# Gated-attention loop on one core: residual adds on GpSimd, half of every second turned copy on ScalarE, moments one step later

## The chip, the cores and the metric

One Trainium2 chip, of which one core is used. A core has TensorE (PE: matmuls, its weight loads are listed as PEld), VectorE (DVE), ScalarE (ACT), GpSimd (POOL) and SyncE (SP, which issues the DMAs here); they run their own instruction streams, in order, and meet at semaphores. The metric is the device time of one execution of the whole kernel in microseconds (us), as a median of runs. Durations come from one profiled execution, whose trace lists every instruction by engine and by line of the kernel.

## What is computed

Four blocks in a row, each with a residual and a layer norm: a linear attention, a gated attention with one shared key and value head per token, a decay attention and a grouped attention with a routed mixture of experts. The change lies in the second:

```python
gating = softmax(x @ W_gate.T); idx = argmax(gating)          # 16 heads
k_shared, v_shared = key head idx, value head idx * max(gating)
att = einsum('bhqd,bkd->bhqk', q, k_shared) / sqrt(hd)         # hd = 16
att = softmax(where(causal, att, -inf))
y = einsum('bhqk,bkd->bhqd', att, v_shared)
x = layernorm(x + y)
```

There are 4 batches of 256 tokens and 256 features, so 1024 tokens in 8 tiles of 128.

## The kernel before

`layer0_gated_attention` first makes the gates, picks keys and values (token tiles `kv_tok`), and spreads and turns the keys. Its main part is a loop over 32 steps of two heads each (8 steps per batch) and two loops of overhang; each engine has its own copy of the loop, written out by hand, and the order in an engine's copy is the order of its queue. For step `n`:

- PE writes a causal mask (`masks`, L942) and scores (`scores`, L956 and L958) of both heads into two PSUM banks, 0 and 1 or 2 and 3 in turn.
- DVE takes the negated maxima of the rows (`maxima`, L785 and L786).
- ACT takes four exponentials into `probs` (`exps`, L868).
- PE turns the probabilities with six transposes (`turn`, L949) into banks 4 and 5, one bank per head, two loops later: loop `n` turns step `n - 2`.
- DVE copies both banks to `probsT` (`copy_turned`, L791), also two loops later. There are 4 buffers of `probsT`, but only one pair of banks, so the next turn waits for the copy.
- In every even loop PE multiplies two steps' turned probabilities with the values (`values`, L968 and L970); a column of ones in the values gives the sum of the probabilities.

Every fourth loop ACT copies a half batch of results out (`copy_out`, L874), and at the loops `out_at(b, t)`, which are 12, 14, 20, 22, 29 and 30 for the first three batches, PE turns a token tile of results (`turn_outputs`, L978) and DVE runs `outputs`: a reciprocal (L797), the product with it (L799) and the sum with the residual `x` into `y` (L801). Right behind each, DVE takes the moments of that tile for the next norm (L547). The norm of the first four tiles runs inside the loop as well: variance in loop 22 (L553, L561), its power on POOL (L615), factors and products in loop 24, and transposes, high and low parts in loops 25 to 28.

POOL makes paddings and prepares weights of the next layer (`following.prepare`), then only the power. Behind the loop ACT loads the Silu table (L892), evaluates queries of the next layer (L1140, L1142) and copies the last results out, for whose transposes PE waits. The last two tiles have their `outputs` there. A barrier ends the block; the next layer starts behind it.

Of the kernel before, what the change touches and what calls it, by code (L numbers as in the profile page):

```python
# [23 lines left out]
ALU = mybir.AluOpType  # L24
ACT = mybir.ActivationFunctionType
# [5 lines left out]
BATCH, SEQ, D = 4, 256, 256  # L31
# [3 lines left out]
TPB = SEQ // P  # L35
CAUSAL = 384

H0, HD0 = 16, 16
# [63 lines left out]
def need(eng, sem, value):  # L102
    if value > 0:
        eng.wait_ge(sem, value)
# [556 lines left out]
def layer0_gated_attention(c, norm, following, next_norm, later_norm):  # L661

    nc, ps = c.nc, c.ps
# [4 lines left out]
    STEPS = BATCH * PER  # L668
# [3 lines left out]
    with ExitStack() as ctx:  # L672
        def sb(name, shape, dt=F32):
# [20 lines left out]
            ctx, "g", "z_ps lg_ps kv_ps q_ps kT_ps s_ps t_ps pv_ps o_turned")  # L694
        z_ready, picked_ps, kv_ready, nm_ready, pT_ready, rs_ready, o_scaled, chain = c.sems(
            ctx, "g", "z_ready picked_ps kv_ready nm_ready pT_ready rs_ready o_scaled chain")
        z_copied, e_ready, q_ready, k_ready, kT_ready, p_ready, o_ready = c.sems(
            ctx, "g", "z_copied e_ready q_ready k_ready kT_ready p_ready o_ready")
        c.finished += pe_sems
        block = ctx.enter_context(nc.Block())  # L700

# [2 lines left out]
        def out_at(b, t):  # L704
            return PER * b + (13 + t if b == 2 else 12 + 2 * t)
# [22 lines left out]
        @block.gpsimd  # L728
        def _(pool):
            norm.split(pool, 1)  # L730
            pool.memset(kv_tok[:], 0.0).then_inc(padded, 1)
            pool.memset(k_pad[:], 0.0).then_inc(padded, 1)
            pool.wait_ge(padded, 1)
            pool.memset(kv_tok[:, :, 1, HD0:HD0 + 1], 1.0).then_inc(padded, 1)
            following.prepare(pool)
            next_norm.power(pool)

        @block.vector
        def _(dve):
            norm.moments(dve, range(6, NT))  # L740
            norm.variance(dve, 1)
            norm.factors(dve, 1)
            norm.apply(dve, 1)
            norm.low(dve, 1)
            link = Chain(dve, chain)

            z, e, cand, one_hot, top_hot, eq = (gate[:, n] for n in range(6))
            nmax, esum, emax, erec, top, first = (gstat[:, n] for n in range(6))

            def wide(a):  # L750
                return a.unsqueeze(2).broadcast_to((P, NT, H0))

            dve.wait_ge(lg_ps, 1)
            logits = ps[:, 0, 0:NT * H0].rearrange("p (t h) -> p t h", t=NT)
            link(dve.tensor_reduce(nmax, logits, X, ALU.max, negate=True))
            dve.tensor_tensor(z, logits, wide(nmax), ALU.add).then_inc(z_ready, 1)
            dve.wait_ge(e_ready, 1)
            dve.tensor_reduce(esum, e, X, ALU.add)
            link(dve.tensor_reduce(emax, e, X, ALU.max))
            link(dve.reciprocal(erec, esum))  # L760
            dve.tensor_tensor(top, emax, erec, ALU.mult)

            link(dve.tensor_tensor(eq, e, wide(emax), ALU.is_equal))
            link(dve.scalar_tensor_tensor(cand, eq, -16.0, c.iota.unsqueeze(1).broadcast_to((P, NT, H0)), ALU.mult, ALU.add))
            link(dve.tensor_reduce(first, cand, X, ALU.min))
            link(dve.tensor_tensor(one_hot, cand, wide(first), ALU.is_equal))
            link(dve.tensor_tensor(top_hot, one_hot, wide(top), ALU.mult))
            dve.wait_ge(padded, 3)

            def pick(t):  # L770
                dve.wait_ge(kv_ps, t + 1)
                kv = kv_bank(t).rearrange("p (a h d) -> p a h d", a=2, h=H0)
                for a, hot in enumerate((one_hot, top_hot)):
                    mul = dve.tensor_tensor(picked[:, t % 2, a], kv[:, a], hot[:, t, :].unsqueeze(2).broadcast_to((P, H0, HD0)), ALU.mult)
                mul.then_inc(picked_ps, 1)

            def gather(t):
                dve.wait_ge(picked_ps, t + 1)
                dve.tensor_reduce(kv_tok[:, t, :, 0:HD0], picked[:, t % 2].rearrange("p a h d -> p a d h"), X, ALU.add).then_inc(kv_ready, 1)

            def maxima(n):
                dve.wait_ge(s_ps, n + 1)
                need(dve, p_ready, n - 3)
                pair = ps[:, banks(n):banks(n) + 2, :]
                dve.tensor_reduce(neg_max[:, n % 4, 0], pair[:, :, 0:P], X, ALU.max, negate=True)  # L785
                dve.tensor_reduce(neg_max[:, n % 4, 1], pair[:, :, P:CAUSAL], X, ALU.max, negate=True).then_inc(nm_ready, 1)  # L786

            def copy_turned(n):
                dve.wait_ge(t_ps, n + 1)
                need(dve, pv_ps, (n - KEPT_T) // 2 + 1)  # L790
                dve.tensor_copy(probsT[:, n % KEPT_T], ps[:, 4:6, 0:CAUSAL]).then_inc(pT_ready, 1)  # L791

            def outputs(b, t):
                seq = TPB * b + t
                turned = out_bank(b, t).rearrange("p (h r) -> p h r", h=H0)
                dve.wait_ge(o_turned, seq + 1)
                dve.reciprocal(rsum[:, t, :], turned[:, :, HD0]).then_inc(rs_ready, 1)  # L797
                dve.wait_ge(rs_ready, seq + 1)
                dve.tensor_tensor(o_tok[:, t], turned[:, :, 0:HD0], rsum[:, t, :].unsqueeze(2).broadcast_to((P, H0, HD0)), ALU.mult).then_inc(o_scaled, 1)  # L799
                dve.wait_ge(o_scaled, seq + 1)  # L800
                dve.tensor_tensor(c.y[:, seq, :], o_tok[:, t].rearrange("p h d -> p (h d)"), c.x[:, seq, :], ALU.add).then_inc(y_ready, 1)  # L801

            for t in range(NT):
                pick(t)
                gather(t)
            for n in range(STEPS + 2):
                if n < STEPS:
                    maxima(n)
                if n >= 2:
                    copy_turned(n - 2)  # L810
                if n in (TURN_AT + 1, TURN_AT + 3):
                    next_norm.low(dve, 0, [(n - TURN_AT - 1) // 2])
                for b in range(BATCH - 1):
                    for t in range(TPB):
                        if n == out_at(b, t):
                            outputs(b, t)
                            dve.wait_ge(y_ready, TPB * b + t + 1)
                            next_norm.moments(dve, [TPB * b + t])
                if n == TURN_AT - 3:
                    next_norm.variance(dve, 0)  # L820
                if n == TURN_AT - 1:
                    next_norm.factors(dve, 0)
                    next_norm.apply(dve, 0)
            following.low_queries(dve, 0)
            for t in range(TPB):
                outputs(BATCH - 1, t)
            following.low_keys(dve, 0)

        @block.scalar
        def _(act):  # L830
# [2 lines left out]
            norm.apply_act(act, 1)  # L833
            def gates_out(n):
                act.wait_ge(z_ps, n + 1)
                act.activation(z_T[:, n * 512:(n + 1) * 512], ps[0:H0, 5 * n, :], ACT.Copy).then_inc(z_copied, 1)

            def queries_out(i):
                half, m = query_order[i]
# [23 lines left out]
            def exps(n):  # L863
# [4 lines left out]
                        ex = act.activation(probs[:, n % KEPT, i, cols], ps[:, banks(n) + i, cols], ACT.Exp, bias=neg_max[:, n % 4, t, i:i + 1])  # L868
                ex.then_inc(p_ready, 1)

            def copy_out(half):
                act.wait_ge(pv_ps, 2 * half + 2)
                need(act, o_turned, half // 2 * TPB)
                act.activation(o_sb[:, half % 2, :], ps[:, 6, :], ACT.Copy).then_inc(o_ready, 1)  # L874
# [6 lines left out]
                spread_keys(t)  # L881
            for n in range(STEPS):
                exps(n)
                if n in (3, 5):
                    turned_keys(1, (n - 3) // 2)
                if n >= 6 and (n - 6) % 4 == 0:
                    copy_out((n - 6) // 4)
                if n == TURN_AT - 1:
                    next_norm.apply_act(act, 0)
                if n in (TURN_AT, TURN_AT + 2):  # L890
                    next_norm.high(act, 0, [(n - TURN_AT) // 2])
            act.activation(following.table[:], c.iota[:, 0:1], ACT.Silu)  # L892
            following.queries_out(act, 0, 0)
            copy_out(2 * BATCH - 1)
# [4 lines left out]
        def _(pe):  # L899
# [22 lines left out]
            norm.split(pe, 1)  # L922
            gates_in(1)
            queries_in(1, 0)
            pe.wait_ge(z_copied, 2)
            for t in range(NT):
                mm = pe.transpose(ps[:, 0, t * H0:(t + 1) * H0], z_T[:, t * P:(t + 1) * P], c.ident[0:H0, 0:H0])
            mm.then_inc(lg_ps, 1)
# [15 lines left out]
            def turn(n):  # L944
                pe.wait_ge(p_ready, n + 1)
                need(pe, pT_ready, n)
                for i in range(2):
                    for k in range(3):
                        mm = pe.transpose(ps[:, 4 + i, k * P:(k + 1) * P], probs[:, n % KEPT, i, k * P:(k + 1) * P], c.ident)  # L949
                mm.then_inc(t_ps, 1)  # L950
# [9 lines left out]

            def values(quad):
                pe.wait_ge(pT_ready, 2 * quad + 2)
                need(pe, o_ready, quad // 2)
                b = quad // 4
                out = ps[:, 6, quad % 2 * SEQ:(quad % 2 + 1) * SEQ]
# [1662 lines left out]
```

## Time and profile before

| | |
|---|---|
| median of 3 runs | 965.43 us (965.05 to 967.98) |
| profiled execution: its time, its span in the trace | 968.8 us, 967.0 us |
| PE busy in the span | 894.3 us (92%) |
| DVE busy | 654.6 us (68%) |
| POOL busy | 455.8 us (47%) |
| ACT busy | 416.8 us (43%) |
| the loop in the trace | about 123 to 210 us |

The page of the profile gives busy time by engine, and the trace behind it can be asked for waits (who idled until whom), for groups of instructions by line, and for the timeline. In a timeline row the columns are start, duration (of the merged run of instructions), engine, line, operation and tiles; a bracket at the end is the idle time ahead of it and who ended it. Matmuls are pipelined, so the start marks tell more of PE than its busy share.

### The profile page before, as it was taken

Reading aid. Unit: us, or ns where it says so; the run is one execution under the profiler, and the core shown is the slowest. Engines: PE = TensorE matmul, PEld = TensorE weight load, DVE = VectorE, ACT = ScalarE, POOL = GpSimd, SP = SyncE. Lnnn points to the kernel's source line nnn. Section 1 sums busy time; section 2 is a strip of 40 time slices with the busy share of each in tenths; the row PEclk is TensorE's granted clock in tenths of the full one; section 3 lists DMA queues with packets and bytes.
Section 4 is the critical chain, followed back from the end, with each engine's and each line's share of the span. In section 5 each row is a group of like instructions: output and inputs, shape, how many; then the busy total and the mean of one; then the engine's idle time right before and its main releaser. Section 6 shows DMA issues by size and latency. Waiting matters only on the chain. (4 is left out here: it accounts for less than half of the span.)

```text
span 967.0 us, 17722 instructions
## 1 busy us (share of the span) xinstructions
PE 894.3 (92%) x6526; PEld 731.5 (76%) x6536; DVE 654.6 (68%) x1154; ACT 416.8 (43%) x1002; POOL 455.8 (47%) x409
## 2 busy tenths in 40 slices
PE   9998999988999999999999879999999978899970
PEld 5566666767888888888888668888888955788860
DVE  3577678975566675576665689778888758476436
ACT  4323456643544545445455345434232444233322
POOL 2000400015667766776766255554545414888405
PEclk9999999999999999999999899999999999999995
DMA  5000200004433433333332101131000031664014
GB/s 194 1 2 2 66 1 2 2 19 122 150 110 101 124 109 105 89 105 119 104 109 62 55 12 50 45 103 40 1 2 1 1 126 37 240 242 137 28 41 124
DMA packets 53459, 72.05 MB, mean 75 GB/s; under 512 B 4992, under 2 KB 45056, under 8 KB 52224
## 3 DMA queue, kind: packets, MB, share of 16 engines
q1 hardware_dynamic: 51840, 66.72, 21.8%
q0 software_dynamic: 1536, 4.20, 1.4%
q8 instruction: 55, 0.90, 0.4%
q14 instruction: 28, 0.23, 0.1%
HBM read 61.73 MB, written 9.18 MB: 73 GB/s over the span
## 5 line engine op out<-in xcount | busy, mean ns | idle before, releaser
L1765 ACT ACTIVATE e_probs<-ps,e_neg_max 128x256 f32<-128x256 f32 (+1 forms) x128 | 52.1, 419 | 121.9 <-DVE e_neg_max L1691 121.9
L125 PE MATMUL ps<-xTl,d_wh 128*128 128x512 f32 x192 | 80.8, 421 | 2.8 <-DVE d_s_m L1281 2.8
L1281 DVE TENSOR_TENSOR d_s_m<-ps,d_decay 128x768 f32<-128x768 f32 x64 | 58.3, 952 | 34.4 <-PE ps L1443 32.1
L1644 POOL TENSOR_TENSOR e_q_T<-xT 128x512 f32<-128x512 f32 x32 | 41.1, 1284 | 82.0 <-DVE xT L1679 82.0
L1086 POOL TENSOR_TENSOR d_wh<-d_stage,d_nought 128x512 fp32r<-128x512 f32 x32 | 43.2, 1351 | 75.8 <-PE ps L125 33.1
L125 PE MATMUL ps<-xTh,d_wh 128*128 128x512 f32 x192 | 76.3, 397 | 0.0
L125 PE MATMUL ps<-xTh,d_wl 128*128 128x512 f32 x192 | 76.1, 396 | 0.0
L615 POOL TENSOR_TENSOR n_rstd<-n_var,half_power 128x4 f32<-128x4 f32 x6 | 6.1, 1023 | 133.5 <-DVE n_var L561 133.4
L1360 ACT ACTIVATE d_gated_hi<-d_gated 128x512 fp32r<-128x512 f32 x32 | 20.2, 632 | 108.6 <-DVE d_gated L1287 108.6
L125 PE MATMUL ps<-f_wl,wh_gated 128*128 (+2 forms) x184 | 65.2, 354 | 1.9 <-DVE f_rows L2237 0.7
L125 PE MATMUL ps<-f_wh,wh_gated 128*128 (+2 forms) x184 | 62.8, 341 | 0.0
L125 PE MATMUL ps<-f_wh,wl_gated 128*128 (+2 forms) x184 | 62.6, 340 | 0.0
L868 ACT ACTIVATE g_probs<-ps,g_neg_max 128x256 f32<-128x256 f32 (+1 forms) x128 | 43.2, 422 | 31.6 <-DVE g_neg_max L786 31.1
L1157 DVE TENSOR_TENSOR wl_gated<-d_q_T,wh_gated 128x512 fp32r<-128x512 f32 x32 | 22.7, 710 | 50.0 <-ACT wh_gated L1142 50.0
L1650 POOL TENSOR_TENSOR e_probs<-e_probs,e_rsum 128x256 f32<-128x256 f32 x64 | 52.5, 841 | 6.8 <-DVE e_rsum L1696 6.8
L1094 POOL TENSOR_TENSOR d_wh<-d_stage,d_nought 128x256 fp32r<-128x256 f32 x32 | 26.9, 839 | 48.2 <-PE ps L125 48.0
L1272 POOL TENSOR_TENSOR d_sq_sum<-d_sq_sum,d_sq 128x512 f32<-128x512 f32 x32 | 44.2, 1382 | 10.6 <-ACT d_sq L1364 10.6
L125 PEld LDWEIGHTS ps<-xTl,d_wh 128*128 128x128 f32 x192 | 36.4, 190 | 15.7 <-issue 8.8
L1088 POOL TENSOR_TENSOR d_wl<-d_stage,d_wh 128x512 fp32r<-128x512 f32 x32 | 43.3, 1352 | 2.5
L2126 POOL TENSOR_TENSOR f_wl<-f_stage,f_wh 128x1024 fp32r<-128x1024 f32 x18 | 43.3, 2435 | 0.0
L125 PEld LDWEIGHTS ps<-xTh,d_wh 128*128 128x128 f32 x192 | 36.4, 189 | 9.0
L125 PEld LDWEIGHTS ps<-xTh,d_wl 128*128 128x128 f32 x192 | 36.5, 190 | 7.1
(389 smaller groups left out, 2894.3 us busy)
## 6 DMA issues: line engine op xcount, KB each, us to landing
d_decay<-in_decay SPq DMA_DIRECT2D x32, 384.0 KB, 3.8
f_stage<-in_w_experts SPq DMA_DIRECT2D x8, 1536.0 KB, 7.1
d_stage<-in_w_decay SPq DMA_DIRECT2D x32, 256.0 KB, 3.0
d_stage<-in_w_decay SPq DMA_DIRECT2D x32, 128.5 KB, 3.4
d_stage_v<-in_w_decay SPq DMA_DIRECT2D x32, 128.0 KB, 2.3
d_stage<-in_w_decay SPq DMA_DIRECT2D x32, 128.0 KB, 2.4
slot_rows<-warm SPq DMA_DIRECT2D x1, 2944.0 KB, 10.5
slot_outs<-f_rows SPq DMA_DIRECT2D x23, 128.0 KB, 3.2
```

Source lines behind the costliest of these rows:

```text
L125: mm = pe.matmul(out, w(k), x(k), start=(opens and n == 0), stop=(closes and n == 3 * len(ks) - 1))
L868: ex = act.activation(probs[:, n % KEPT, i, cols], ps[:, banks(n) + i, cols], ACT.Exp, bias=neg_max[:, n % 4, t, i:i + 1])
L1086: pool.tensor_tensor(wh, qk, self.nought[:].unsqueeze(1).broadcast_to((P, KD, 2 * P)), ALU.add).then_inc(self.qk_high, 1)
L1088: pool.tensor_tensor(wl, qk, wh.bitcast(F32), ALU.subtract).then_inc(self.qk_split, 1)
L1094: pool.tensor_tensor(wh, g, self.nought[:].unsqueeze(1).broadcast_to((P, KD, P)), ALU.add).then_inc(self.g_high, 1)
L1157: dve.tensor_tensor(self.q_lo, self.q_T[:], self.q_hi.bitcast(F32), ALU.subtract).then_inc(self.qk_lo, 1)
L1272: pool.tensor_tensor(sq_sum[:, cols], sq_sum[:, cols], sq[:], ALU.add).then_inc(sq_added, 1)
L1281: dve.tensor_tensor(s_m[:, s % 2, 2 * b:2 * b + 2, :], ps[:, 2 + 2 * b:4 + 2 * b, 0:CAUSAL], decay[:], ALU.mult).then_inc(sm_ready, 1)
L1644: pool.tensor_tensor(dst, by_cos[:, n % 2, :], by_sin[:, n % 2, :], ALU.add).then_inc(roped, 1)
L1650: mul = pool.tensor_tensor(part, part, rsum[:, s % 4, t, :].unsqueeze(2).broadcast_to((P, 2, cols.stop - cols.start)), ALU.mult)
L1765: ex = act.activation(probs[:, s % KEPT, i, cols], ps[:, 2 + i, cols], ACT.Exp, bias=neg_max[:, s % 4, t, i:i + 1], accum_out=sums[:, s % ...
L2126: low = pool.tensor_tensor(wl[:, cols], stage[e % 2][:, PARTS[n]], wh[:, cols].bitcast(F32), ALU.subtract)
```

## The change

POOL does the residual add of the six tiles of the first three batches, behind its weights, with the norm's power between the fourth and the fifth add; the product of a later tile on DVE waits for the add that frees its buffer. The moments move to the loop behind each output, and the variance from loop 22 to loop 23. Of every odd step's turned probabilities, DVE copies the first head's bank and ACT the second's, behind its exponentials of that loop, and behind the whole loop for the last step. A semaphore that counted gate copies counts ACT's halves too, and PE waits for it ahead of turns and values.

```diff
+            def add(seq):
+                pool.wait_ge(o_scaled, seq + 1)
+                pool.tensor_tensor(c.y[:, seq, :], o_tok[:, seq % TPB].rearrange("p h d -> p (h d)"), c.x[:, seq, :], ALU.add).then_inc(y_ready, 1)
+
+            for seq in range(2 * TPB):
+                add(seq)
             next_norm.power(pool)
+            for seq in range(2 * TPB, 3 * TPB):
+                add(seq)
...
             def copy_turned(n):
                 dve.wait_ge(t_ps, n + 1)
                 need(dve, pv_ps, (n - KEPT_T) // 2 + 1)
-                dve.tensor_copy(probsT[:, n % KEPT_T], ps[:, 4:6, 0:CAUSAL]).then_inc(pT_ready, 1)
+                if n % 2 == 0:
+                    dve.tensor_copy(probsT[:, n % KEPT_T], ps[:, 4:6, 0:CAUSAL]).then_inc(pT_ready, 1)
+                else:
+                    dve.tensor_copy(probsT[:, n % KEPT_T, 0], ps[:, 4, 0:CAUSAL]).then_inc(pT_ready, 1)
...
+                need(dve, y_ready, seq - TPB + 1)
                 dve.tensor_tensor(o_tok[:, t], turned[:, :, 0:HD0], rsum[:, t, :].unsqueeze(2).broadcast_to((P, H0, HD0)), ALU.mult).then_inc(o_scaled, 1)
-                dve.wait_ge(o_scaled, seq + 1)
-                dve.tensor_tensor(c.y[:, seq, :], o_tok[:, t].rearrange("p h d -> p (h d)"), c.x[:, seq, :], ALU.add).then_inc(y_ready, 1)
+                if b == BATCH - 1:
+                    dve.wait_ge(o_scaled, seq + 1)
+                    dve.tensor_tensor(c.y[:, seq, :], o_tok[:, t].rearrange("p h d -> p (h d)"), c.x[:, seq, :], ALU.add).then_inc(y_ready, 1)
...
                         if n == out_at(b, t):
                             outputs(b, t)
+                        if n == out_at(b, t) + 1:
                             dve.wait_ge(y_ready, TPB * b + t + 1)
                             next_norm.moments(dve, [TPB * b + t])
-                if n == TURN_AT - 3:
+                if n == TURN_AT - 2:
                     next_norm.variance(dve, 0)
...
+            def copy_turned(n):
+                act.wait_ge(t_ps, n + 1)
+                need(act, pv_ps, (n - KEPT_T) // 2 + 1)
+                act.activation(probsT[:, n % KEPT_T, 1], ps[:, 5, 0:CAUSAL], ACT.Copy).then_inc(act_copied, 1)
...
             for n in range(STEPS):
                 exps(n)
+                if n >= 2 and n % 2 == 1:
+                    copy_turned(n - 2)
                 if n in (3, 5):
                     turned_keys(1, (n - 3) // 2)
...
+            copy_turned(STEPS - 1)
             act.activation(following.table[:], c.iota[:, 0:1], ACT.Silu)
             following.queries_out(act, 0, 0)
             copy_out(2 * BATCH - 1)
...
             def turn(n):
                 pe.wait_ge(p_ready, n + 1)
                 need(pe, pT_ready, n)
+                need(pe, act_copied, 2 + n // 2 if n >= 2 else 0)
...
             def values(quad):
                 pe.wait_ge(pT_ready, 2 * quad + 2)
+                pe.wait_ge(act_copied, 2 + quad + 1)
                 need(pe, o_ready, quad // 2)
```

## Rows read from the trace of the kernel before

**Rows 1.** Waits from 123 to 213 us: total us, times, longest us.

```profile
POOL n_rstd L615 <- DVE n_var L561: 70.1, 1, 70.1
ACT g_probs L868 <- DVE g_neg_max L786: 31.1, 30, 2.2
DVE g_neg_max L785 <- PE ps L958: 10.3, 14, 1.8
...
PE ps L949 <- DVE g_probsT L791: 3.4, 12, 0.8
...
PEld ps L968 <- issue: 2.5, 15, 0.2
```

**Rows 2.** Timeline of loops 7 and 8, and ACT in loop 6.

```profile
137.78 1.35 ACT L868 ACTIVATE g_probs<-ps,g_neg_max 128x128 f32<-128x128 f32 x4 [0.47 <-DVE g_neg_max L786]
...
138.14 0.39 PE L942 MATMUL ps<-neg,ident 128*128 128x256 bf16 x2
...
139.00 0.61 ACT L874 ACTIVATE g_o_sb<-ps 128x512 f32<-128x512 f32 x1
...
139.43 0.42 DVE L785 TENSOR_REDUCE g_neg_max<-ps 128x2 f32<-128x256 f32 x1 [0.88 <-PE ps L958]
...
140.37 0.95 DVE L791 COPY g_probsT<-ps 128x768 f32<-128x768 f32 x1
140.54 1.35 ACT L868 ACTIVATE g_probs<-ps,g_neg_max 128x128 f32<-128x128 f32 x4 [0.93 <-DVE g_neg_max L786]
...
141.46 0.84 PE L949 MATMUL ps<-consts,g_probs 128*128 128x128 f32 x6 [0.20 <-DVE g_probsT L791]
...
143.03 0.39 PE L942 MATMUL ps<-neg,ident 128*128 128x256 bf16 x2
```

**Rows 3.** Groups by line and shape: busy us, mean ns, idle before.

```profile
L349 ACT ACTIVATE a_o_sq<-ps 128x256 f32<-128x256 f32 x8 | 2.9, 379 | 4.4 <-PE ps L450 4.3
...
L1094 POOL TENSOR_TENSOR d_wh<-d_stage,d_nought 128x256 fp32r<-128x256 f32 x32 | 26.9, 839 | 48.2 <-PE ps L125 48.0
```

**Rows 4.** Timeline: start marks of loops 3, 4, 23, 25, 30 and 31.

```profile
129.02 0.42 DVE L785 TENSOR_REDUCE g_neg_max<-ps 128x2 f32<-128x256 f32 x1
...
131.46 0.87 PE L949 MATMUL ps<-consts,g_probs 128*128 128x128 f32 x6
...
179.00 0.39 PE L942 MATMUL ps<-neg,ident 128*128 128x256 bf16 x2
...
184.50 0.39 PE L942 MATMUL ps<-neg,ident 128*128 128x256 bf16 x2
...
198.15 0.88 PE L949 MATMUL ps<-consts,g_probs 128*128 128x128 f32 x6
...
200.18 0.39 PE L942 MATMUL ps<-neg,ident 128*128 128x256 bf16 x2
```

**Rows 5.** Timeline of the loop's end, from the turn of step 30.

```profile
204.64 0.85 PE L949 MATMUL ps<-consts,g_probs 128*128 128x128 f32 x6 [0.35 <-DVE g_probsT L791]
...
205.10 1.28 ACT L892 ACT_TABLE_LOAD   x1
...
206.63 0.85 PE L949 MATMUL ps<-consts,g_probs 128*128 128x128 f32 x6 [0.35 <-DVE g_probsT L791]
...
207.11 0.63 ACT L1142 ACTIVATE wh_gated<-d_q_T 128x512 fp32r<-128x512 f32 x1
...
209.45 0.60 ACT L874 ACTIVATE g_o_sb<-ps 128x512 f32<-128x512 f32 x1 [1.70 <-PE ps L970]
...
210.15 1.07 PE L978 MATMUL ps<-consts,g_o_sb 128*128 128x128 f32 x8
```

**Rows 6.** Windows: length, busy time (instructions) by engine, PEclk, DMA share, GB/s.

```profile
88.00:92.00 4.00, 2.39 (x12) 1.66 (x13) 2.96 (x7) 1.89 (x4) 0.00 (x0) 1.00 0.00 0
...
218.00:219.00 1.00, 0.00 (x0) 0.00 (x0) 0.86 (x1) 0.00 (x0) 0.85 (x2) 1.00 0.41 142
...
220.00:221.00 1.00, 0.90 (x2) 0.83 (x3) 1.00 (x5) 0.00 (x0) 0.00 (x0) 0.50 0.27 25
```

More of the change, by code:

```diff
@@ L696, in layer0_gated_attention @@
             ctx, "g", "z_ready picked_ps kv_ready nm_ready pT_ready rs_ready o_scaled chain")
-        z_copied, e_ready, q_ready, k_ready, kT_ready, p_ready, o_ready = c.sems(
-            ctx, "g", "z_copied e_ready q_ready k_ready kT_ready p_ready o_ready")
+        act_copied, e_ready, q_ready, k_ready, kT_ready, p_ready, o_ready = c.sems(
+            ctx, "g", "act_copied e_ready q_ready k_ready kT_ready p_ready o_ready")
         c.finished += pe_sems
@@ L835, in gates_out @@
                 act.wait_ge(z_ps, n + 1)
-                act.activation(z_T[:, n * 512:(n + 1) * 512], ps[0:H0, 5 * n, :], ACT.Copy).then_inc(z_copied, 1)
+                act.activation(z_T[:, n * 512:(n + 1) * 512], ps[0:H0, 5 * n, :], ACT.Copy).then_inc(act_copied, 1)
             def queries_out(i):
@@ L924, in _ @@
             queries_in(1, 0)
-            pe.wait_ge(z_copied, 2)
+            pe.wait_ge(act_copied, 2)
             for t in range(NT):
```

## Prediction, made before the changed kernel was run

> **What bounds the kernel now.** I read the table of waits of the gated loop first, then the timeline of one pair of steps, then the start marks of the other pairs, then the loop's end. In the waits the reader is to see three things [rows 1]. ACT idles 31.1 us ahead of its exponentials, each time until VectorE (DVE) has the negated maxima. DVE idles 10.3 us until TensorE (PE) has the scores. PE idles only 3.4 us, in 12 places, all of them at the transposes, until DVE has copied the turned probabilities. GpSimd (POOL) stands still for 70.1 us. So PE sets the pace, and 3.4 us is nearly all that faster neighbours can give it.
>
> The order of PE is fixed: a pair is an odd loop (masks, scores, turn of the step two earlier) and an even loop (masks, scores, turn, values). The pair of loops 7 and 8 shows what closes the circle [rows 2]. PE begins masks of loop 7 at 138.14; its scores let DVE's maxima start at 139.43, 1.29 later. DVE then copies turned step 5 from 140.37 to 141.32, and PE's turn of step 6, which overwrites the same two PSUM banks, starts at 141.46 after an idle of 0.20. That is 2.03 after the maxima's start. Masks of loop 9 follow at 143.03, 1.57 later. 1.29 + 2.03 + 1.57 = 4.89 is the pair. ACT starts the exponentials of loop 7 at 140.54, 1.11 after the maxima's start, and needs 1.35 for the four. They are beside this path: what waits for them comes a loop later.
>
> **The change part by part.**
>
> *The ACT half of the odd copies* is what decides. It takes bank 5 of each odd step from DVE and queues it on ACT. Its place in ACT's order is behind the exponentials of the same loop: in loop 7, the exponentials of step 7, then the copy of step 5. The new wait on PE stands ahead of the turn of every even step, and the turn of step 6 needs exactly that copy. What is queued behind this wait on PE is the rest of the loop: turn, values, masks and scores of the next loop, and so the next maxima and exponentials. So the path, from the maxima's start, becomes: 1.11 to the exponentials; their 1.35 less an overlap of 0.13 (in loop 6 the output copy started at 139.00, when the exponentials begun at 137.78 were 0.13 short of their end [rows 2]); the copy itself; and the hand-over to PE. The trace has no ACT copy of 128x384 from PSUM. Its ends are 0.38 (a square of 128x256 from PSUM [rows 3]) and 0.61 (the copy of 128x512 [rows 2]); I take 0.50, half way in elements. The hand-over from ACT to PE took 0.10 (the output copy ended at 209.45 + 0.60, the transposes began at 210.15 [rows 5]); DVE's took 0.14 [rows 2], which is the other end. Sum: 1.11 + 1.22 + 0.50 + 0.10 = 2.93 where it was 2.03. An undisturbed pair grows by 0.90, to 5.79. Nothing on the way can start sooner: the maxima wait for scores, the scores for PE's order.
>
> *The DVE half* ends some 0.4 earlier than the full copy of 0.95 [rows 2], as an estimate from half its elements. That would end the 0.20 idle, but ACT's half now comes 0.90 later than the full copy did, so it is worth nothing. The Trainium skill says otherwise in spirit: its page "Perfetto Trace Analysis", section "Identifying the Most-Contended Engine", has the engine with the highest occupancy optimized first, and among the engines that feed PE here that is DVE. By that alone the sum would be the 3.4 us of PE's waits back. The trace disagrees, since DVE itself waits for PE; it is the rival of the other sign below.
>
> *Six residual adds on POOL* and *moments one loop later*: costed at nothing, and worth nothing on DVE, which waits for PE. An add of this shape takes POOL at most 0.84 (its nearest row of 128x256 [rows 3]); POOL has nothing else to do, as its 70.1 us wait shows [rows 1], and its only queued item, the power of the norm, stands between adds 4 and 5 whose inputs come in that order. The wait for the sum stands on DVE behind the next loop's maxima and copy, about 1.5 after the product; maxima queue behind it. If that cover were gone, each of six places could hold DVE up by at most 0.84, some 5 in all, and only what passes ACT's half would show. DVE had been late for PE around the variance (the longest of PE's waits, 0.8 [rows 1]); this goes away, but what is late next there is ACT's copy.
>
> *The variance one loop later* moves to loop 23; POOL's power must return within a loop. Nothing. *The added waits on PE*: 32 ahead of turns and 16 ahead of values. Most lie inside a stall; I take nothing, and as the other end what PE's weight loads idled for issue ahead of the values, which have two waits, 2.5 us over 15 [rows 1], 0.17 each: 48 of them are 8 us. The turns, with two waits too, idled in only 12 of 32 places [rows 1], so I stay at nothing.
>
> **The sum**, against the profiled execution (968.8, span 967.0, 3.4 above the median of the runs):
> - Loops 3 to 6: the turn of step 2 moves from 131.46 to 129.02 + 2.93 = 131.95 [rows 4], +0.49. From it to masks of loop 7 were 138.14 - 131.46 = 6.68, and will be 1.57 + 5.79 = 7.36: +0.68.
> - Loops 7 to 22, eight pairs, from 138.14 [rows 2] to 179.00 [rows 4], 40.86 us: in each the turn waits for the DVE copy, in pairs with outputs too (these add PE work behind the turn, before and after alike). 8 x 0.90 = +7.20.
> - Loops 23 and 24: 184.50 - 179.00 = 5.50 [rows 4], which had the late variance in it; now 5.79: +0.29.
> - Loops 25 to 30: 200.18 - 184.50 = 15.68 [rows 4], with extra transposes on PE that had covered the copy. Now 5.79 twice, and for the last pair, whose output transposes make it 200.18 - 198.15 = 2.03 from turn to masks, 1.29 + 2.93 + 2.03 = 6.25: 17.83, +2.15.
> - The end [rows 5]. Before, from masks of loop 31 (200.18) to the last output transposes (210.15): 9.97. ACT did its Silu table load at 205.10, right behind the last exponentials and beside PE. Now the copy of step 31 stands ahead of the load and waits for the last turn. From masks 31: turn of step 30 at 4.22; turn of step 31 1.99 later (206.63 - 204.64), 6.21; its six transposes 0.85; copy 0.50 and 0.03 to start, 7.59; load to the second query activation 2.01 (207.11 - 205.10), 9.60; that one 0.63, the output copy 0.60 with 0.13 overlap, 10.70; hand-over 0.10: 10.80. +0.83. Everything behind, into the next layer, follows this.
>
> 0.49 + 0.68 + 7.20 + 0.29 + 2.15 + 0.83 = **+11.6**: span 978.6, and on the median 965.43 + 11.6 = **977.0**.
>
> **The rivals.**
>
> *A, the halves come in time (faster).* If ACT's half were done when PE reaches the turn, PE's 3.4 us of waits go [rows 1]: about 962.0. For it: ACT has 31.1 us of idle ahead of its exponentials, far more than sixteen copies of 0.50. Against: that idle lies ahead of the exponentials, and the copy is behind them. It decides at a copy done about 1.0 earlier than I have it, before the exponentials are through. 0.04, and 0.03 for something between, within 0.3% of the time before, which is about what a measurement of this kernel can tell from no change.
>
> *B, the clock falls.* PE will idle some 0.9 longer in each pair, 1.1 in one piece. The granted clock was 0.50 (1.2 GHz) from 220 to 221, with PE idle from 218 to 219 ahead of it [rows 6]; it stayed at 1.00 (2.4 GHz) from 88 to 92, where PE was busy for 2.39 of 4 us [rows 6]. The Trainium skill, "TensorE: Matmul & The Clock Gate", section "What's actually happening", says that the throttled clock is the default and that activity releases it; the rows agree. At half clock a pair would be 2 x 1.29 + 2.93 + 2 x 1.57 = 8.65, 2.86 more in 14 pairs, 40 in all: about 1017. Against it: PE stays busy for some 4.7 of 5.79 us, a larger share than in that stretch. 0.03.
>
> *C, PE's new waits cost issue time,* up to 8 us for 48 of them: up to 985, likelier half of that, 981. 0.08.
>
> **How the numbers follow.** The forecast, ACT's half behind the exponentials, has 0.82. Its own bounds: the copy at 0.38 or 0.61 moves 14 pairs by 1.6 either way, DVE's hand-over and no overlap add up to 2.4, and the runs before spread from 0.4 below to 2.6 above their median. So 973 to 982, which takes in the likelier half of C. Slower 0.93 (forecast, B, C), same 0.03, faster 0.04.
>
> **What the profile would show.** Right: PE's idle ahead of the even turns near 1.1 to 1.2 us, released by ACT's new copy; 16 such copies near 0.50; masks of odd loops 5.8 apart; ACT's wait ahead of the exponentials unchanged or longer; the table load near 8 us behind masks 31. Wrong: turns released by DVE or not waiting, a copy that runs ahead of the exponentials, or a granted clock under 1.00 in the loop. DVE waiting for POOL's sums would make the adds' cover wrong.

## The result and the profile after

The changed kernel took 981.35 us (median of three runs, 980.63 to 982.08), the kernel before 965.24 beside it: a ratio of 1.016, interval 1.0134 to 1.0187, slower. A fourth run took 1489.89 with a mean granted clock of 0.554 and is left out; with it the median is 981.72. The profiled execution took 980.63, with a span of 978.4.

The table of waits of the changed loop, 121.96 to 221.23 us (total us, times, longest us; PE's turn is now L973, DVE's maxima L794, ACT's exponentials L883 and ACT's new copy L889), answers to [rows 1]:

```profile
POOL y L739 <- DVE g_o_tok L812: 94.6, 6, 47.0
ACT g_probs L883 <- DVE g_neg_max L795: 31.9, 20, 3.1
DVE g_neg_max L794 <- PE ps L982: 18.5, 25, 1.8
...
PE ps L973 <- ACT g_probsT L889: 14.1, 15, 1.2
...
ACT g_probsT L889 <- PE ps L973: 3.0, 1, 3.0
```

PE's idle ahead of the turns has a new releaser, ACT's copy, and is 14.1 us where it was 3.4. DVE waits longer for PE, 18.5 us where it was 10.3: the work that was taken from it did not make PE's path shorter. ACT idles ahead of its exponentials as before; its copies did not fill that idle. No wait of DVE for POOL's sums is listed.

The timeline of loops 7 and 8, the counterpart of [rows 2]:

```profile
137.99 0.39 PE L965 MATMUL ps<-neg,ident 128*128 128x256 bf16 x2
...
139.28 0.42 DVE L794 TENSOR_REDUCE g_neg_max<-ps 128x2 f32<-128x256 f32 x1 [1.02 <-PE ps L982]
...
140.22 0.55 DVE L803 COPY g_probsT<-ps 128x384 f32<-128x384 f32 x1
140.39 1.35 ACT L883 ACTIVATE g_probs<-ps,g_neg_max 128x128 f32<-128x128 f32 x4 [1.68 <-DVE g_neg_max L795]
...
141.62 0.51 ACT L889 ACTIVATE g_probsT<-ps 128x384 f32<-128x384 f32 x1
...
142.27 0.84 PE L973 MATMUL ps<-consts,g_probs 128*128 128x128 f32 x6 [1.17 <-ACT g_probsT L889]
...
143.84 0.39 PE L965 MATMUL ps<-neg,ident 128*128 128x256 bf16 x2
```

The reader is to see the circle: maxima at 139.28, exponentials 1.11 later, ACT's copy 1.23 behind their start, 0.51 long, then 0.14 to PE. DVE's half, done at 140.77, has been waiting for 1.5 us when the turn starts. The pair is 143.84 - 137.99 = 5.85; it was 4.89.

The end, counterpart of [rows 5]:

```profile
214.67 0.85 PE L973 MATMUL ps<-consts,g_probs 128*128 128x128 f32 x6 [0.17 <-ACT g_probsT L889]
...
216.61 0.85 PE L973 MATMUL ps<-consts,g_probs 128*128 128x128 f32 x6 [0.31 <-issue]
...
217.49 0.49 ACT L889 ACTIVATE g_probsT<-ps 128x384 f32<-128x384 f32 x1 [2.97 <-PE ps L973]
218.00 1.28 ACT L915 ACT_TABLE_LOAD   x1
...
220.55 0.58 ACT L894 ACTIVATE g_o_sb<-ps 128x512 f32<-128x512 f32 x1
...
221.23 1.07 PE L1003 MATMUL ps<-consts,g_o_sb 128*128 128x128 f32 x8 [1.37 <-issue]
```

ACT stands for 2.97 us ahead of the last copy, and the table load, which ran beside PE before, starts behind it.

The start marks of masks and of the last output transposes give the stretches of the loop in every trace. They repeat closely (two executions of the changed kernel differ by 0.01 us in any of these), far better than whole executions do.

| us | before | changed | adds only | ACT half only | copy first | and last on DVE | copied twice |
|---|---|---|---|---|---|---|---|
| loops 3 to 6 | 10.40 | 11.69 | 10.40 | 11.70 | 10.39 | 10.40 | 12.46 |
| 7 to 22 | 40.86 | 48.55 | 40.86 | 48.58 | 38.90 | 38.90 | 54.66 |
| 23, 24 | 5.50 | 5.85 | 4.89 | 6.47 | 4.65 | 4.64 | 6.24 |
| 25 to 30 | 15.68 | 17.99 | 16.55 | 18.00 | 16.40 | 16.40 | 19.14 |
| 31 and the end | 9.97 | 10.85 | 9.43 | 10.86 | 10.49 | 9.38 | 11.61 |
| first maxima to last output transposes | 86.74 | 99.27 | 86.47 | 99.95 | 85.18 | 84.05 | 108.45 |

### The profile page after: what moved, and what is told of

Same layout as the page of the kernel before. It is cut to its first block and busy times, and to the rows that moved or that the text cites. A ratio compares the mean times of both kernels' runs of the same rounds, so it can differ in the third digit from the quotient of the medians.

```text
span 978.4 us, 17770 instructions
## 1 busy us (share of the span) xinstructions
PE 894.0 (91%) x6536; PEld 730.4 (75%) x6536; DVE 646.3 (66%) x1148; ACT 423.6 (43%) x1018; POOL 459.7 (47%) x415
## 5 line engine op out<-in xcount | busy, mean ns | idle before, releaser
L883 ACT ACTIVATE g_probs<-ps,g_neg_max 128x256 f32<-128x256 f32 (+1 forms) x128 | 43.2, 422 | 33.3 <-DVE g_neg_max L795 31.9
L739 POOL TENSOR_TENSOR y<-g_o_tok,x 128x256 f32<-128x256 f32 x6 | 4.3, 724 | 94.6 <-DVE g_o_tok L812 94.6
```

## The experiments

The theory on trial: ACT's half stands behind the exponentials in ACT's order, and PE waits for it ahead of every even turn. Rivals: the adds on POOL cost it; a copy on ACT costs wherever it stands; something outside the loop takes part.

**The adds without ACT's half.** DVE copies both banks again, the waits on PE go:

```diff
-                if n % 2 == 0:
-                    dve.tensor_copy(probsT[:, n % KEPT_T], ps[:, 4:6, 0:CAUSAL]).then_inc(pT_ready, 1)
-                else:
-                    dve.tensor_copy(probsT[:, n % KEPT_T, 0], ps[:, 4, 0:CAUSAL]).then_inc(pT_ready, 1)
+                dve.tensor_copy(probsT[:, n % KEPT_T], ps[:, 4:6, 0:CAUSAL]).then_inc(pT_ready, 1)
...
-                if n >= 2 and n % 2 == 1:
-                    copy_turned(n - 2)
...
-                need(pe, act_copied, 2 + n // 2 if n >= 2 else 0)
...
-                pe.wait_ge(act_copied, 2 + quad + 1)
```

> The POOL adds and the later moments and variance stay; both banks of every step are copied by DVE as before, with the waits of before. Order theory (ACT's half stands behind the exponentials and closes PE's circle): all of the loss is gone, pairs are 4.89 us again, the late maxima around the variance only move by a loop, so 964 to 966, within 0.3% of the kernel before, and the turns wait for DVE some 3 us in all. Adds rival (the slower adds on POOL hold up DVE and with it PE): most of the 16 us stays, 975 or more, and DVE shows waits for the sums.

966.16 against 966.27, a ratio of 0.9999 (0.998 to 1.0017): no change that can be told. In this kernel's table of waits PE's turn L966 waits for DVE's copy as before:

```profile
PE ps L966 <- DVE g_probsT L800: 2.4, 11, 0.4
```

The adds rival falls. The start marks show what the change does without ACT's half: the pair of loops 23 and 24 is 0.61 shorter, the pair of loops 25 and 26 longer, 5.95 for 5.08, and the end 0.54 shorter. The stall at the variance has moved: moments and variance now stand on DVE between the copy of loop 23 and the maxima of loop 24, ACT's exponentials wait for these maxima, and behind the exponentials ACT scales two norm tiles, for which PE's transposes wait (timeline, same kernel):

```profile
186.77 0.63 PE L648 MATMUL ps<-consts,x 128*128 128x128 f32 x4 [0.68 <-ACT x L625]
```

**ACT's half without the adds.** POOL's adds go back to DVE, moments and variance to their loops:

```diff
...
-            for seq in range(2 * TPB):
-                add(seq)
             next_norm.power(pool)
-            for seq in range(2 * TPB, 3 * TPB):
-                add(seq)
...
-                if b == BATCH - 1:
+                if True:
...
-                        if n == out_at(b, t) + 1:
...
-                if n == TURN_AT - 2:
+                if n == TURN_AT - 3:
                     next_norm.variance(dve, 0)
```

> Only ACT's half of the odd copies, its place and its waits; adds, moments and variance as before. Order theory: pairs of 5.85 us as in the changed kernel, and as the path now goes through the odd maxima, DVE's extra work in the output loops shows too: 0.6 at the variance and 0.1 to 0.2 in five other places, 1.3 in all, so 982 to 983.5, slower than the change. Adds rival: 966 to 968. If both parts cost, something between.

979.9, a ratio of 1.0128 (1.0109 to 1.0147). The half alone brings the loss, as the order theory has it. That the adds with the later moments and variance help it a little is seen in the trace alone: 0.68 in the loop, all but 0.06 of it at the variance, where DVE's maxima come 0.6 late and the circle passes it on:

```profile
188.36 0.42 DVE L785 TENSOR_REDUCE g_neg_max<-ps 128x2 f32<-128x256 f32 x1
...
191.36 0.84 PE L962 MATMUL ps<-consts,g_probs 128*128 128x128 f32 x6 [1.79 <-ACT g_probsT L878]
```

The five other places of 0.1 to 0.2 did not show, and the time lies under the 982 to 983.5 that was expected: a miss in size.

**The copy ahead of the exponentials.** Two lines of ACT's loop change places:

```diff
-                exps(n)
                 if n >= 2 and n % 2 == 1:
                     copy_turned(n - 2)
+                exps(n)
```

> The change with one order turned round on ACT: in each odd loop the half copy of the step two earlier stands ahead of the exponentials, not behind them. Order theory: ACT's half is done some 0.3 us before PE reaches the even turn, which then waits for nobody; plain pairs take 4.61, 0.28 under the kernel before; with the end still 0.8 longer by the copy ahead of the table load, 2.1 under the kernel before in the loop, 963. Any-copy rival (a copy on ACT costs wherever it stands, by its hand-over and PE's new waits): above 970. If the waits on PE cost issue time, plain pairs stay near 4.9 with an idle put down to issue.

965.63, a ratio of 0.9987 (0.9972 to 1.0002). The same copies on the same engine, with the same waits on PE, and the loss is gone. The timeline of loops 7 and 8 of this kernel:

```profile
139.47 0.43 DVE L794 TENSOR_REDUCE g_neg_max<-ps 128x2 f32<-128x256 f32 x1 [0.88 <-PE ps L982]
...
140.27 0.49 ACT L889 ACTIVATE g_probsT<-ps 128x384 f32<-128x384 f32 x1 [0.60 <-PE ps L973]
...
140.41 0.55 DVE L803 COPY g_probsT<-ps 128x384 f32<-128x384 f32 x1
140.66 1.35 ACT L883 ACTIVATE g_probs<-ps,g_neg_max 128x128 f32<-128x128 f32 x4
...
141.23 0.87 PE L973 MATMUL ps<-consts,g_probs 128*128 128x128 f32 x6
```

ACT copies in what had been its idle time, the exponentials start 1.19 instead of 1.11 behind the maxima, and the turn follows with no idle: the pair is 4.65, expected 4.61. The loop is 1.56 shorter than before, expected 2.1; the pair of loops 25 and 26, at 5.80 where it was 5.08, is more than the difference. In whole runs this gain cannot be told from no change. So neither the hand-over nor PE's added waits are a price worth naming, and the rival of a copy that costs anywhere falls.

**And the last step on DVE.**

```diff
-                if n % 2 == 0:
+                if n % 2 == 0 or n == STEPS - 1:
...
-            copy_turned(STEPS - 1)
...
-                pe.wait_ge(act_copied, 2 + quad + 1)
+                pe.wait_ge(act_copied, 2 + min(quad + 1, QUADS - 1))
```

> As the kernel with the copy ahead of the exponentials, and the last step's both banks on DVE, so that ACT's table load doesn't wait for the last turn. Order theory: another 1.1 less at the end, 962, faster than the kernel before by 0.3%. If the end has slack that the sum missed, the same as the kernel with the copy first.

963.25, a ratio of 0.9951 (0.9932 to 0.9971): faster than both kernels. The end is 9.38 for 10.49, 1.11 less, as expected. The loop is 84.05, 2.7 us under the kernel before; the ratio makes it 4.7 us, and the 2 us between them have no place in the loop.

**Every ACT half twice,** the first to a spare tile:

```diff
+                need(act, padded, 3 + n // 2)
+                act.activation(spare[:], ps[:, 5, 0:CAUSAL], ACT.Copy).then_inc(padded, 1)
                 act.activation(probsT[:, n % KEPT_T, 1], ps[:, 5, 0:CAUSAL], ACT.Copy).then_inc(act_copied, 1)
```

> The change with every ACT half copied twice, first to a spare tile, with its own semaphore count. Order theory: the second copy starts some 0.4 behind the first and lies wholly on PE's path, so every pair that waits for it grows by 0.4, from 5.85 to 6.25, fourteen pairs and the end by 6.0 in all: about 105.2 us from the first maxima to the last output transposes instead of 99.3. If ACT's copy were beside the path, or the loss came with the waits alone, under 1 us.

989.15 in one run; the loop 108.45, not 105.2. Plain pairs are 6.24, as expected for a copy wholly on the path. What was not expected are two pairs of 7.55: PE's clock fell in them, which with the two pairs behind them makes 3.0 of the 3.25 us. The windows of this kernel, one us each (length, busy time of PE, PEld, DVE, ACT, POOL, then the granted clock), and the turn there:

```profile
149.00:150.00 1.00, 0.59 (x8) 0.38 (x4) 0.61 (x3) 1.00 (x4) 0.00 (x0) 1.00 0.00 0
150.00:151.00 1.00, 0.00 (x0) 0.00 (x0) 0.66 (x2) 1.00 (x4) 0.00 (x0) 1.00 0.00 0
151.00:152.00 1.00, 0.86 (x4) 0.89 (x5) 0.00 (x0) 1.00 (x4) 0.00 (x0) 0.54 0.00 0
152.00:153.00 1.00, 1.00 (x8) 0.46 (x10) 0.30 (x1) 0.25 (x1) 0.00 (x0) 0.50 0.06 16
```

```profile
151.14 1.51 PE L976 MATMUL ps<-consts,g_probs 128*128 128x128 f32 x6 [1.55 <-ACT g_probsT L892]
```

**The changed kernel once more,** without an edit, for the size.

> The changed kernel once more, against the kernel before in the same minutes, for the size of the loss: its first timing gave 16 us, while in the two traces the loop and its end are 12.5 longer and the rest 1.1 shorter. Order theory: 12.5, a ratio of 1.013, with the same marks in the loop to 0.1 us, and what differs outside the loop changes from execution to execution without a place of its own. Outside rival (the change costs a further 3 to 4 us somewhere behind the loop): 1.0165 again, and one stage behind the loop is longer in this trace too.

980.89 against 966.27, a ratio of 1.0147 (1.0122 to 1.0171). The loop is 99.27 again. The 12.5 us that it accounts for, 1.013, lie inside this interval and just under that of the first timing; the outside rival's 1.0165 lies inside both. The rest of the span, outside the stretch of the table, is 879.1 and 879.6 in the two executions of the changed kernel, 880.3 in the kernel before, and from 876.5 to 882.7 over the traces of the others. From the last output transposes to the end of the span are 757.2 and 756.2 us in the changed kernel and 756.9 in the kernel before, so the traces do not bear the outside rival out. That a last 2 to 3 us belong to the change is not shown, and not excluded.

**Two norm tiles on POOL,** on top of the fastest version:

```diff
             next_norm.power(pool)
+            pool.wait_ge(next_norm.rstd_ready, next_norm.so["rstd_ready"] + 1)
+            next_norm.apply(pool, 0)
...
                     next_norm.factors(dve, 0)
-                    next_norm.apply(dve, 0)
```

> The kernel with the copy first and the last step on DVE, and also the two token tiles of the norm that DVE scaled in loop 24 on POOL. In that kernel loops 25 and 26 take 5.81 where 5.08 was reached before, as DVE comes late to its maxima. If that is DVE's work on the norm, the pair falls back to 5.1 to 5.2, the stretch from the first maxima to the last output transposes from 84.05 to 83.4, the time to 962.5 beside 963.2. If POOL is too slow for it (0.7 each and more), PE's norm transposes wait and the pair stays at 5.5 or more.

964.37, a ratio of 0.9977 (0.9953 to 1.0001), and the pair of loops 25 and 26 is longer still, 6.06; the loop is 84.34. POOL needs 1.2 us for each of the two tiles, which DVE scales in 0.73 together, and PE waits for it (timeline, same kernel):

```profile
184.97 2.45 POOL L591 TENSOR_SCALAR x<-y,n_mv,n_rstd 128x256 f32<-128x256 f32 x2
...
187.51 0.63 PE L648 MATMUL ps<-consts,x 128*128 128x128 f32 x4 [0.80 <-POOL x L591]
```

The expectation had also taken the wrong piece of DVE's work. In the kernel without this edit (timeline of the copy first and the last step on DVE):

```profile
180.89 0.17 DVE L561 TENSOR_SCALAR n_var<-n_mv 128x4 f32<-128x4 f32 x1
180.97 0.42 DVE L794 TENSOR_REDUCE g_neg_max<-ps 128x2 f32<-128x256 f32 x1
...
182.08 1.35 ACT L883 ACTIVATE g_probs<-ps,g_neg_max 128x128 f32<-128x128 f32 x4 [0.93 <-DVE g_neg_max L795]
...
182.84 0.73 DVE L591 TENSOR_SCALAR x<-y,n_mv,n_rstd 128x256 f32<-128x256 f32 x2
...
183.31 1.10 ACT L625 ACTIVATE x<-y,n_shift,n_rstd 128x256 f32<-128x256 f32 x2
...
184.55 0.63 PE L648 MATMUL ps<-consts,x 128*128 128x128 f32 x4 [0.53 <-ACT x L625]
```

PE's norm transposes wait for ACT's two tiles, these stand behind ACT's exponentials, and the exponentials waited 0.93 for maxima that DVE took right behind the variance. DVE's own two tiles come behind those maxima, so moving them could not make the maxima earlier. This is read from the trace; no run moved the moments or the variance alone.

## Why the prediction was right, and where its size was off

The direction and the mechanism were right: what decides is the place of ACT's half, behind the exponentials. The experiment that turns that order round takes the loss away, the one that keeps only the half keeps it, and the one that doubles the copy adds to it.

By its steps:
- *An undisturbed pair grows by 0.90, to 5.79.* It grew to 5.85. The copy took 0.51 for 0.50, and the hand-over 0.14, the other end that was named, where 0.10 was taken; the overlap was 0.12. That is the term that was mis-sized, by 0.06 in each pair.
- *The sum of 11.6.* The loop and its end grew by 12.5, and the mis-sized pair is most of the difference. Loops 3 to 6: 1.29 for 1.17. The eight pairs: 7.69 for 7.20. Loops 23 and 24: 0.35 for 0.29. Loops 25 to 30: 2.31 for 2.15. The end: 0.88 for 0.83.
- *The time, 977.0.* It came 4.4 higher (981.35), near the top of the range. 0.9 of that is the loop. The rest is not in it: the two timings put the loss at 15.4 and 14.2 us by their ratios, and only the second interval takes in the loop's 12.5. The rest of the span moves by 6 us from trace to trace. The range took it in because it had been widened for such a spread and for half of rival C, not because a step accounts for it. The forecast of the span, 978.6 beside 978.4, is closer than its working deserves: in that trace the loop is 0.9 longer than forecast and the rest 1.1 shorter than before, which is luck.
- *The adds on POOL, costed at nothing.* Right: 0.72 us each, no wait of DVE for them, and no change in the time by themselves.
- *The variance one loop later, nothing.* Right in the changed kernel, as the longer loop covers it. In a loop without the loss it costs 0.7 to 0.9 at the norm's transposes, beside the 0.6 that it saves at the variance: the cover was the loss itself.
- *Added waits on PE, nothing.* Right: from masks to the odd turn 1.17 us before and after; from the even turn to values 0.78 and 0.77. Rival C falls.
- *Rival A, the halves in time.* It asked for a copy ahead of the exponentials, which is what the two-line experiment makes of it; its 3.4 us less were nearly reached (2.7 in the loop) once the last step went back to DVE.
- *Rival B, the clock.* It did not fall in the changed loop, with PE idle for 1.17 in one piece. It did in two places of the doubled copy, at 1.55, and there the two pairs took 1.3 longer, less than the 2.86 that the rival counted for a pair wholly at half clock. So the danger was real. How near the changed loop came to it is not shown: seven other turns of the doubled copy waited 1.55 too and ran at full clock, and so did the one turn that waited 1.79 in the kernel with ACT's half alone.

The Trainium skill's page "Perfetto Trace Analysis", section "Identifying the Most-Contended Engine", has the engine with the highest occupancy optimized first. Here the trace disagrees with it in the changed kernel: of the engines that feed PE, DVE was the busiest, its busy time in this stretch fell from 72.3 to 63.8 us, and the stretch grew by 12.5. With the copy first and the last step on DVE, DVE is busy for 62.9 us and the stretch is 2.7 shorter than before: between these two kernels relieving DVE cost time where PE had to wait for the work in its new place, and paid where it did not.

## What to carry to other kernels

When work is moved to an engine with idle time, look at where in that engine's order the idle lies: ACT had 31 us ahead of its exponentials, and the copy was queued behind that instruction. Add up the circle through the new place (what the engine must finish first, the moved work, the hand-over) and compare it with the moment at which the bound engine asks for the result. Try both orders before giving up the move: here, in the loop and with the rest of the change, the same copies cost 12.5 us behind the exponentials and saved 1.6 ahead of them, 2.7 with the last one left where it was.

## What was not expected of the hardware

The granted clock fell in a loop that kept PE busy for most of the time. In the kernel with the doubled copy nine turns waited 1.55 us for ACT. Two of them ran at a granted clock of 0.50 to 0.54, the lower level of 1.2 GHz (six transposes in 1.51 us instead of 0.85), and the clock was back at 1.00 some 3 us later; the other seven, with the same idle ahead of them, ran in 0.84 to 0.85. In the two traces of the changed kernel, with waits of 1.17, no turn was slow, and a single wait of 1.79 in the kernel with ACT's half alone left the clock at 1.00. What sets the two turns apart is not shown.

POOL took 1.2 us to scale a tile of 128x256 with two operands per partition, where it adds two such tiles in 0.72.
